# A two-layer relational graph network on one core: reciprocals of the counts on ten partitions, the last batch of nodes in two parts, and the rows of h stored by ScalarE

## What is computed

```python
def _rgcn_layer(x, src, dst, edge_type, w_rel, root, bias):
    seg = dst * NUM_REL + edge_type
    xs = x[src]
    sums = segment_sum(xs, seg, N * NUM_REL)
    cnt = segment_sum(ones, seg, N * NUM_REL)
    mean = (sums / maximum(cnt, 1.0)[:, None]).reshape(N, NUM_REL, -1)
    return einsum('nrd,rdo->no', mean, w_rel) + x @ root + bias
edge_type = argmax(msg[:, 16:-16], axis=1)
h = relu(_rgcn_layer(x, src, dst, edge_type, w_rel1, root1, b1))
x = layernorm(x + _rgcn_layer(h, src, dst, edge_type, w_rel2, root2, b2))
```

## Time and profile before

| | before |
|---|---|
| median of 3 runs | 4082.41 us (4081.56 to 4084.16) |
| profiled execution: its time, its span | 4082.89 us, 4081.2 us |
| POOL busy | 2974.2 us (73%) |
| DVE busy | 3307.1 us (81%) |
| PE busy | 2501.1 us (61%) |
| ACT busy | 404.8 us (10%) |

### The profile page before, as it was taken

One profiled execution on the slowest core, in us unless ns is written; L12 is line 12 of the kernel. 1 busy time (PEld: TensorE's weight loads), 2 busy tenths in 40 slices (PEclk: granted clock), 3 DMA queues, 4 the chain that ended last, 5 costly groups with the idle time before them and its releaser, 6 DMA issues.

```text
span 4081.2 us, 32441 instructions
## 1 busy us (share of the span) xinstructions
PE 2501.1 (61%) x10787; PEld 1745.1 (43%) x10788; DVE 3307.1 (81%) x2238; ACT 404.8 (10%) x417; POOL 2974.2 (73%) x3144
## 2 busy tenths in 40 slices
PE   3666576767667676767635656556565656565554
PEld 3444354544445454544334434434343434344442
DVE  5787988888888888888827888787878888887877
ACT  1010010101010010101100101101010101010101
POOL 7777777777777777777367777777777777777772
PEclk7667676767777676767766777767676777776775
DMA  4223222222222222222112222222222222222220
GB/s 124 75 72 91 71 90 72 86 76 74 88 72 90 72 90 71 89 72 65 31 53 59 64 62 62 63 62 62 62 64 62 64 62 64 61 62 64 61 63 24
DMA packets 141839, 282.77 MB, mean 69 GB/s; under 512 B 60471, under 2 KB 75707, under 8 KB 138224
## 3 DMA queue, kind: packets, MB, share of 16 engines
q0 software_dynamic: 100032, 205.07, 17.7%
q1 hardware_dynamic: 38044, 76.44, 5.7%
q10 hardware_dynamic: 3719, 0.73, 0.1%
HBM read 261.77 MB, written 20.25 MB: 69 GB/s over the span
## 4 chain that ended last, share of the span: by engine, by line
POOL 71%; issue 24%; DVE 3%; PE 1%; DMA 0%; POOLq 0%; ACT 0%; DVEq 0%; ACTq 0%
POOL rows L1347 71%; DVE ps_bc L2037 2%; PE ps_agg L1723 1%; PE ps_out L1779 0%; DVE mean L2043 0%; DMA table<-h_s 0%; PE ps_bc L1746 0%; DVE S L1996 0%; POOLq L1384 0%; DVE ring L2009 0%; PE ps_out L1774 0%; PE ps_agg L1718 0%; PE ps_out L1789 0%; DMA rows<-in_x_dram,idx_s 0%; DMA rows<-table,idx_s 0%
## 5 line engine op out<-in xcount | busy, mean ns | idle before, releaser
L1347 POOL DMA_INDIRECT rows<-table,idx_s x1563 | 1478.5, 946 | 547.9 <-issue 476.0
L1347 POOL DMA_INDIRECT rows<-in_x_dram,idx_s x1507 | 1431.0, 950 | 459.2 <-issue 459.2
L2037 DVE RECIPROCAL ps_bc<-ps_bc 128x896 f32<-128x896 f32 (+1 forms) x280 | 1606.1, 5736 | 8.4 <-PE ps_bc L1746 8.4
L1723 PE MATMUL ps_agg<-S,rows 128*128 128x130 f32 (+3 forms) x6256 | 1515.0, 391 | 0.0
L1723 PEld LDWEIGHTS ps_agg<-S,rows 128*128 128x128 f32 x6256 | 1254.1, 243 | 158.9 <-issue 80.2
L2009 DVE TENSOR_TENSOR ring<-ps_agg,ring 128x429 f32 (+1 forms) x782 | 455.1, 582 | 529.9 <-PE ps_agg L1723 293.2
L1746 PE MATMUL ps_bc<-cnt_b,sel 10*128 10x448 bf16 (+1 forms) x560 | 236.9, 520 | 967.4 <-DVE mean L2043 963.2
L1996 DVE TENSOR_TENSOR S<-ps_iota,comb_b 128x1600 f32<-128x1600 f32 x392 | 711.4, 1815 | 135.5 <-issue 135.0
L1718 PE MATMUL ps_agg<-zero_b 128*128 128x429 bf16 (+1 forms) x782 | 321.0, 410 | 547.4 <-DMA rows<-table,idx_s 383.9
L1779 PE MATMUL ps_out<-mean,wall 128*128 128x448 f32 (+1 forms) x1120 | 550.8, 620 | 6.7 <-DVE mean L2043 6.7
L1746 PEld LDWEIGHTS ps_bc<-cnt_b,sel 10*128 10x128 bf16 x560 | 34.3, 102 | 1085.9 <-DVE mean L2043 1068.2
(11 more groups left out here) (112 smaller groups left out, 550.7 us busy)
## 6 DMA issues: line engine op xcount, KB each, us to landing
attr<-in_edge_attr_dram SPq DMA_DIRECT2D x27, 1176.0 KB
rows<-table,idx_s POOLq DMA_INDIRECT x1563, 2.5
rows<-in_x_dram,idx_s POOLq DMA_INDIRECT x1507, 2.5
x_in<-in_x_dram SPq DMA_DIRECT2D x54, 224.0 KB
table<-outT SPq DMA_DIRECT2D x27, 224.0 KB, 2.0
table<-h_s SPq DMA_DIRECT2D x27, 224.0 KB
xt_s<-table SPq DMA_DIRECT2D x27, 224.0 KB
out_dram<-h_s SPq DMA_DIRECT2D x27, 224.0 KB
```

Of the source, the lines that this page charges most:

```text
L1347: pool.indirect_dma_start(out=rows[:, o, j, :], out_offset=None, in_=(x, htab)[l][:, :], in_offset=bass.IndirectOffsetOnAxis(ap=at, axis=0 ...
L1723: ins = t_.matmul(sums[:, :, lo:lo + w], lhsT=rows[:, o, jj, :], rhs=S[:, (par + o) % 2, jj, :].rearrange("p (r n) -> p r n", n=WN)[:, :, ...
L2037: v_.reciprocal(two, two).then_inc(rc_done[k], 1)
```

## The change

**Reciprocals.** `clamp` and `divide` go. In the first layer `reciprocals` takes max(count, 1) on ten partitions, its reciprocal in f32, and splits that into three bf16 parts that stand on partitions 0 to 9, 32 to 41 and 64 to 73 of `rc_b` (74 rows, the others zero). `sel` has 74 rows too, so that one product of `spread` adds the three parts. `scale` is then the product of `ps_bc` with the ring alone. The second layer reads `rc_b` from memory.

**The last batch** is finished in two parts, EARLY (192 nodes) and LATE (212). The early part's work stands between the octs 4 to 6 of batch 27, the late part's behind them. It has tiles of its own (`x_end`, `z_end`, `stat_end`) and uses the two banks of `ps_agg[0]`.

**Order of the other work.** Spreads and transforms of a full batch begin half an oct to an oct earlier, and `turn_back` comes at quad (4, 1) instead of the end of oct 6. `make_types` moves to oct 2; `centre` and `spread_of` to octs 5 and 6.

**The store of h.** ScalarE issues it itself, behind its copy to `h_s` (or `z_end`). SP keeps the other stores and loads, and loads `x_end` once in each layer.

**The start.** The first 8 tiles' indices are loaded into `idx_0` by a DMA of ScalarE that takes them from memory one by one, and POOL waits for that alone (`first_in`) before its first eight gathers. The constants that POOL made are now made by DVE, five of them ahead of `nat_s`; `place` comes behind `idx_t`.

```diff
+EARLY = 192
+LATE = ENDN - EARLY
+BAND = 32
+CROWS = 2 * BAND + R
-        sel = sb("sel", [R, R, P], BF16)
+        sel = sb("sel", [CROWS, R, P], BF16)
...
+            pool.wait_ge(first_in, 16)
+            for j in range(GT):
+                gather(0, 0, j, idx_0[:, j:j + 1])
             pool.wait_ge(idx_done, 1)
-            for o in range(OCTS):
+            for o in range(1, OCTS):
                 for j in range(GT):
                     gather(0, o, j, idx_t[:, o * GT + j:o * GT + j + 1])
-                if o == 0:
-
-                    g_.memset(eps[:], EPS).then_inc(consts_done, 1)
-                    g_.affine_select(out=sel[:], in_=sel[:], compare_op=ALU.not_equal, fill=1.0, base=0,
-                                     pattern=[[-1, R], [0, P]], channel_multiplier=1).then_inc(consts_done, 1)
-                    g_.memset(hit_typ[:], 0.0).then_inc(consts_done, 1)
-                    g_.memset(zero_b[:], 0.0).then_inc(consts_done, 1)
...
+                save_part(*EARLY_PART, PARTS - 1)
+                save_part(*LATE_PART, PARTS)
+                save_counts(END, PARTS)
+
+                sp.wait_ge(hT_saved, 16 * PARTS)
                 sp.wait_ge(cnt_saved, 16 * HALVES)
...
+                sp.wait_ge(xt_turned, HALVES)
+                load_x_end()
...
+            act.dma_start(idx_0[:, :].bitcast(I32), src[0:GE].rearrange("(t p) -> p t", p=P),
+                          allow_slow_non_contiguous=True).then_inc(first_in, 16)
...
+                    a_.copy(to[0:n // 4, :, :].rearrange("p c d -> p (c d)"), bank[0:n // 4, :]).then_inc(h_ready, 1)
+                    act.wait_ge(h_ready, made)
...
+                    act.dma_start(part_rows(htab, b, lo, n), to[0:n // 4, :, :]).then_inc(rows_saved, 16)
...
+                SPREADS = {(1, 0): 0, (1, 1): 1, (2, 0): 2, (2, 1): 3, (3, 0): 4}
+                TYPES = {(2, 0): (-1, 0, 1), (2, 1): (2, 3), (3, 0): (4, 5), (3, 1): (6, 7), (4, 0): (8, 9)}
+
+                END_SPREADS = {(4, 1): (0,), (5, 0): (1, 2), (5, 1): (3, 4)}
+                END_TYPES = {(5, 1): (-1, 0, 1, 2, 3)}
...
+                def reciprocals(par, lo, n, made, last_made, saved):
+
+                    f0, f1 = (f[:, 0:n] for f in rc_f)
...
+                    v_.tensor_scalar(f0, ring[0:R, R, par * HN + lo:par * HN + lo + n], 1.0, None, ALU.max
+                                     ).then_inc(rc_step[0], 1)
+                    dve.wait_ge(rc_step[0], made)
+                    v_.reciprocal(f1, f0).then_inc(rc_step[1], 1)
+                    dve.wait_ge(rc_step[1], made)
+                    v_.tensor_copy(rc_b[0:R, lo:lo + n], f1).then_inc(rc_step[2], 1)
+                    dve.wait_ge(rc_step[2], made)
+                    v_.tensor_tensor(f0, f1, rc_b[0:R, lo:lo + n], ALU.subtract).then_inc(rc_step[3], 1)
+                    dve.wait_ge(rc_step[3], made)
+                    v_.tensor_copy(rc_b[BAND:BAND + R, lo:lo + n], f0)
+                    v_.tensor_copy(rc_m[:, 0:n], f0).then_inc(rc_step[4], 1)
+                    dve.wait_ge(rc_step[4], made)
+                    v_.tensor_tensor(rc_b[2 * BAND:2 * BAND + R, lo:lo + n], f0, rc_m[:, 0:n], ALU.subtract
                                      ).then_inc(cnt_ready, 1)
...
-                    v_.reciprocal(two, two).then_inc(rc_done[k], 1)
-                    dve.wait_ge(rc_done[k], made)
```

547 lines of the change are left out of this document (289 added, 258 removed).

## The result

| | before | after |
|---|---|---|
| median | 4083.15 us (4081.56 to 4084.16, 4 runs) | 4022.83 us (4021.86 to 4024.45, 4 runs) |
| profiled execution: its time, its span | 4082.89 us, 4081.2 us | 4023.58 us, 4021.9 us |
| POOL busy | 2974.2 us | 2991.2 us (74%) |
| DVE busy | 3307.1 us | 1886.3 us (47%) |

The account below looks back on a forecast made before the run. GpSimd's chain of 3126 gathers, one every 1.25 us, was taken as the bound, with about 165 us around it to gain in. Start -8.9, small steps +8, between the layers -31, end -33: -65, so 4017 us, range 4003 to 4032.

Parts of the forecast that it names:

- The small steps: First layer: seven reciprocal steps on ten partitions lengthen gathers, 0.3 us a batch, +8 us over 28 batches.
- The bound of threefold: Upper end for the small steps' cost in the first layer: the rate of 0.1 raised threefold, 24 us.
- The second layer: First to last gather of the second layer: no change, 0 us, gathers still 946 ns.
- Between the layers: Last gather of first layer to first of second: 41.8 us against 72.9, -31, ends -26 and -38.
- The store of 53 rows on one engine: Late part's store: 53 rows on one DMA engine of 16, 5.1 us, against 1 if spread.
- The company of SyncE's load: Between the layers: load of `x_end` beside the store of h lengthens it by 0 to 4.2 us, taken 3.3.
- The end: Last gather's start to end of span: 42.8 us against 76.0, -33, ends -28 and -39.
- Full speed: Rival: TensorE at full speed in both closings, store without company, small steps free: 4000 us; chance 0.12.
- Full copying time: Rival: first layer's small steps hold a gather for their full copying time, 45 us for 8, 4054; chance 0.05.
- the reciprocal's hold: Rival: reciprocal on SBUF and all seven steps hold first-layer gathers throughout, 160 us for 8, 4169; chance 0.03.
- The rival without a hand-over: Rival: early part stalls the quads, late part starts no sooner; only 26 us go from each end, 4030; chance 0.05.
- the signs that were named: First gather near 5.5, ninth 1.25 behind eighth, gathers 955 and 946 ns, closings 42 and 43 us, 53-row share 0.06.

Follow-up runs that it names:

- 48, 97 and 100 rows: Late-store sizes when the changed kernel's EARLY = 192 became 212, 16 and 4: 4013.85 us, 4683.33 us (another, slower chip) and 4021.81 us.

## Why the prediction was right, and where its terms were off

**The bound** was read rightly: the gathers stay the chain, 1421 us of VectorE's work are worth nothing between them on the first chip, and the gain lies around them. The first gather started at 4.46, near the lower bound of its term. The ninth follows the eighth after 1.25 us, so the hole of 2.8 is gone; the 56 first gathers take 57.9 us against 57.3.

**The small steps** were mis-sized: forecast +8, measured +14.7 in the gathers' busy time, and 16.2 when the steps are taken to PSUM. That the steps hold gathers and the reciprocal does not was right. The rate was wrong. It was taken from the earlier trace rows as 0.1 us for each us of work, by the first layer's 4 ns over the second's; but the second layer's gathers are held too, by 3.7 us in the kernel before. The steps without the reciprocal are 84 us in all (0.39 to 0.62 each, in 29 calls), so it is 14.9 / 84, 0.18. The bound of threefold held it. And a rate is not what lies behind it. The forecast read the earlier trace rows as a gather that ends with the `ahit` product beside it. The operation ahead of that product is the one that held it:

```profile
103.20 0.74 DVE L1969 TENSOR_TENSOR ahit<-attr,amax 128x560 f32<-128x560 f32 x1
```

It ends at 103.94, and the gather at 104.76, 0.82 us later, as in all the others. What an operation costs depends on whether a gather begins while it runs, and it is then all that is left of the operation.

The Trainium skill, SBUF — State Buffer, section "Who interferes with whom", says that copies, casts and tensor_scalar can lock GpSimd out for the whole instruction; by that rule the trace agrees: the casts hold a gather until they end (1.12 us in place of 0.95 above). They do not cost their full time (45 us), because most of them run where no gather begins. The same section reports that tensor_tensor does not stall the writing of descriptors, but has one with both inputs in SBUF contend with what GpSimd reads. Whatever it is that the gathers need, the `ahit` products and the norm's do hold them, 8.9 and 5.1 us that go when one operand lies in PSUM.

**The second layer** was forecast at nothing and lost 5.8 us. This term was missing. The last operation of `centre` and that of `normalise` (0.69 us each, both inputs in SBUF) hold gathers; with the norm in PSUM none is held by them. They are as long and as many before the change, where they cost less. The traces show why: before, 12 gathers began while one of them ran, and lost 2.9 us; in the changed kernel 28 did, and lost 8.3, and with `centre` moved back 24, and lost 8.7. If the gathers' starts, 1.25 us apart, fell at random against 56 such operations, each would cost (0.69 - 0.13) x (0.69 - 0.13) / (2 x 1.25) = 0.13 us and all of them 7 us, by an estimate. So the kernel before was lucky, the changed one is not unusual, and the forecast's 946 ns carried that luck over. What sets where in a gather they fall was not tried by itself.

**Between the layers** the step-by-step count held: the last copy ends 33.9 us after the landing of oct 5 (2015.88 - 1982.0, the zero again 1.2 us ahead of the last gather's start), forecast 33.6, and from there to the gather it is 8.7 where 9.4 was forecast. S for the next layer did become the new wait, ahead of the early part's last scales:

```profile
1993.14 1.81 DVE L2050 TENSOR_TENSOR S<-ps_iota,comb_b 128x1600 f32<-128x1600 f32 x1
1994.87 0.55 DVE L2106 TENSOR_TENSOR mean<-ps_bc,ring 128x384 f32<-128x384 f32 x1
...
1995.47 0.50 PE L1765 MATMUL ps_bc<-rc_b,sel 74*128 74x192 bf16 x2 [3.81 <-DVE mean L2106]
```

The store of 53 rows on one engine was rightly seen, and 48, 97 and 100 rows confirm it. The company of SyncE's load cost 1.7 and not 3.3. The rule of the Trainium skill, DMA: Bandwidth & Descriptors, section "Why a DMA increments its semaphore by 16 and not by 1", would put 48 rows on 16 engines, 100 on ten, and 53 and 97 on one; the times at the end of the program go with it in all four (2.4, 2.9, 7.1 and 10.6 us).

The count followed the split step by step and came out, but that does not show the split's worth: without it the gap is 41.8 us, nearly the same.

**The end** was mis-sized, -33 forecast, -38.1 measured. The windows of the changed kernel give busy time by engine and the granted clock of the two halves of the end, and of its store:

```profile
3985.00:3999.00 14.00, 9.64 (x41) 8.84 (x41) 5.81 (x10) 0.63 (x1) 0.00 (x0) 0.56 0.05 12
3999.00:4010.00 11.00, 8.10 (x48) 6.07 (x46) 7.86 (x14) 2.08 (x5) 0.00 (x0) 1.00 0.07 21
```

```profile
4015.50:4021.50 6.00, 0.00 (x0) 0.00 (x0) 0.00 (x0) 0.00 (x0) 0.00 (x0) 0.50 0.06 18
```

and the timeline its last links:

```profile
4004.88 0.90 PE L1785 MATMUL ps_agg<-mean,wall 128*128 128x212 f32 x4
...
4014.13 0.68 DVE L2140 TENSOR_TENSOR z_end<-z_end,stat_end 53x512 f32<-53x512 f32 x1
```

TensorE had 1.00 in the late half, 2.4 GHz; it had just worked from 3992.8 to 4002.6 with no wait over 0.33 us, and kept that clock over one wait of 2.04. The first half was at 0.56, near the 1.2 GHz, with a wait of 3.7 us in it (ahead of 3992.79) and one of 3.4 ahead of it; the forecast took a value between. Counted from the same zero (3982.7), the quad of oct 6 is over at about 15.6 where 16.3 was forecast, the late spread at 17.7 (20.3), the early `centre` at 21.4 (24.1), the last product at 26.1 (31.1), VectorE's end at 32.1 (37.4). So half of the 5.3 us were gone ahead of the late part, and half in its links: a pair of products takes 0.90 us. The store behind is 7.1, near the 6.6 of the forecast, at a share of 0.06, again one engine.

**The rivals.** Full speed was right at the end and not between the layers, where the first 20 us (1984 to 2004) were at 0.59. Full copying time and the reciprocal's hold are excluded by the rows above. The rival without a hand-over came near the truth in one thing and missed in the other: the split as made brings nothing in the whole time, but without it 31.1 and 42.6 us go from the two closings, not 26 each. That 4017 came within 6 us rests on errors of both signs, which is luck in part: -5.1 at the end, +12.2 in the two layers (6.4 + 5.8), -1.6 elsewhere. Of the signs that were named, the means of the gathers failed (959 and 950 ns where 955 and 946 stood), the first because of the rate and the second because of the missing term.

## What to carry to other kernels

Once an engine is off the chain, its work is priced only by what it does to the one that is on it: here a gather that began while VectorE ran an operation with both inputs in SBUF, or a cast or tensor_scalar from SBUF to SBUF, waited until that operation ended. On average that was 0.13 to 0.21 us for each us of such work (the norm's two products 5.1 for 39, the small steps 14.9 for 84, the types' 8.9 for 42), and nothing that can be seen with an operand in PSUM; a reciprocal cost nothing in either place. An average taken in one kernel need not hold in the next, since it hangs on where the gathers begin. A store that the chain waits for should be cut at a number of partitions that many engines can share, before its issue is moved to another engine: 5 rows fewer were worth more than the whole split without it. And a time around a long row of equal steps can be forecast well link by link; look for the errors in what is multiplied by the number of steps.

## What the runs showed that was not expected

**Two chips on which TensorE's signals come late.** On the third chip the changed kernel takes 17% longer than on the first (4703.88 against 4022.83), and the kernel before 28% (5214.6 against 4083.15); on the second chip the kernel before takes 26% longer. An instruction is as long there as on the first chip: a gather 949 ns, S 1818. What is new is waits that no releaser in the trace explains. These are the greatest in the changed kernel on the third chip: what waited, for what, us in total, times, longest:

```profile
ACT idx_s L1574 <- remote: 1864.2, 46, 105.7
DVE ring L2063 <- remote: 1544.2, 153, 42.6
DVE mean L2106 <- remote: 660.4, 87, 19.1
POOL rows L1367 <- remote: 613.5, 157, 11.7
```

and on the first chip, for the first two:

```profile
ACT idx_s L1574 <- PE ps_agg L1747: 1018.4, 27, 49.5
DVE ring L2063 <- PE ps_agg L1747: 844.0, 196, 13.8
```

So it is not one engine that stands still. ScalarE, VectorE and GpSimd all wait longer, and where ScalarE and VectorE on the first chip wait for a product of TensorE. One such place on the third chip, in the timeline:

```profile
3483.60 1.30 PE L1747 MATMUL ps_agg<-S,rows 128*128 128x130 f32 x8
...
3502.32 1.26 DVE L2063 TENSOR_TENSOR ring<-ps_agg,ring 128x390 f32 x2 [20.65 <-remote]
3503.00 0.94 POOL L1367 DMA_INDIRECT rows<-table,idx_s  x1 [5.05 <-remote]
```

The last sums that the two additions read end at 3484.90 by the trace (ends of products are modelled), and VectorE takes up the first of them at 3502.32; GpSimd, which waits for the buffers of rows that the same products free, goes on 0.7 us behind it. Both wait for the same semaphore of TensorE, and the trace has its update at 3502.20, 21.8 us behind the end of the product that updates it (3480.44). On the first chip such updates follow the product's end within 0.02 us nearly always. So there the chain runs through these waits, TensorE and VectorE (48%, 16% and 21% of it in the changed kernel), and not through the gathers. That is why shorter gathers save nothing, and the change, which takes 1421 us of work off VectorE, saves 511 us there (5214.6 - 4703.9), where it saved 60 on the first. Whether the products are late or only their signals, and why, is not shown by anything in these traces and stays open; so does whether it is the chip or something beside it.
